# Expert tiles with one TensorE signal instead of four, down products two tiles behind, and the late scatters in one block

## What is computed

```python
logits = x @ router_w.T
probs = softmax(logits)
top_w, top_idx = top_k(probs, 2)
w_te = einsum('tk,tke->te', top_w, one_hot(top_idx, 8))
g = einsum('th,eih->tei', x, gate_w)      # I = 352, H = 128
u = einsum('th,eih->tei', x, up_w)
h = silu(g) * u
y = einsum('tei,ehi,te->th', h, down_w, w_te)
out = x + layernorm(y)
```

## Time and profile before

| | us |
|---|---|
| median of three runs (lowest, highest) | 591.68 (590.68, 592.72) |
| profiled execution, its span | 596.4 |
| TensorE busy in the span | 532.1 (89%) |
| ScalarE busy | 395.4 (66%) |
| VectorE busy | 375.9 (63%) |
| POOL busy | 349.7 (59%) |

### The profile page before, as it was taken

One profiled execution on the slowest core, in us unless ns is written; L12 is line 12 of the kernel. 1 busy time (PEld: TensorE's weight loads), 2 busy tenths in 40 slices (PEclk: granted clock), 3 DMA queues, 4 the chain that ended last, 5 costly groups with the idle time before them and its releaser, 6 DMA issues.

```text
span 596.4 us, 14609 instructions
## 1 busy us (share of the span) xinstructions
PE 532.1 (89%) x4952; PEld 395.0 (66%) x4969; DVE 375.9 (63%) x1095; ACT 395.4 (66%) x880; POOL 349.7 (59%) x449
## 2 busy tenths in 40 slices
PE   6989899899899899988899899999976899999981
PEld 5655455556566455655555666889976899999960
DVE  6824583965975947996847877527742365555347
ACT  3388989888978788869788696644531355555425
POOL 6104636545538885357877258487578555565545
PEclk9999999999999999999999999999996799999997
DMA  7245333213213322232734512212122203321174
GB/s 196 76 126 161 111 99 109 74 37 108 80 45 122 102 86 71 77 100 78 201 109 134 132 56 52 59 55 69 55 61 69 55 32 86 88 63 32 33 287 141
DMA packets 47016, 55.62 MB, mean 93 GB/s; under 512 B 7376, under 2 KB 41056, under 8 KB 44784
## 3 DMA queue, kind: packets, MB, share of 16 engines
q1 hardware_dynamic: 42624, 45.76, 26.7%
q0 software_dynamic: 4320, 8.92, 4.5%
HBM read 36.27 MB, written 18.92 MB: 93 GB/s over the span
## 4 chain that ended last, share of the span: by engine, by line
PE 56%; DVE 15%; ACT 10%; POOL 6%; issue 6%; DMA 3%; another core or an unknown queue 3%; DVEq 1%; SPq 0%; ACTq 0%; POOLq 0%
PE SC L871 11%; PE OA L748 9%; PE OA L881 6%; PE M L786 4%; PE M L822 4%; PE SC L730 3%; ACT arena L1015 3%; PE SC L734 2%; PE M L643 2%; DVE SS L1330 2%; PE SC L740 2%; PE M L662 1%; POOL slots L1782 1%; PE M L852 1%
## 5 line engine op out<-in xcount | busy, mean ns | idle before, releaser
L1015 ACT ACTIVATE arena<-SC 128x1024 f32<-128x1024 f32 x160 | 161.9, 1039 | 14.7 <-PE SC L735 11.8
L871 PE MATMUL SC<-arena 128*128 128x128 f32 (+1 forms) x852 | 111.5, 283 | 0.0
L871 PEld LDWEIGHTS SC<-arena 128*128 128x128 f32 (+1 forms) x852 | 104.0, 191 | 0.4 <-issue 0.3
L748 PE MATMUL OA<-arena 128*32 128x256 f32 (+1 forms) x1536 | 88.9, 349 | 6.6 <-DVE arena L455 2.8
L1782 POOL DMA_INDIRECT slots<-XBA,IDX x64 | 72.6, 1134 | 37.0 <-DVE IDX L1455 19.6
L1503 DVE TENSOR_TENSOR arena<-arena,SC 128x256 f32<-128x256 f32 (+1 forms) x142 | 43.7, 348 | 68.6 <-issue 24.6
L881 PE MATMUL OA<-arena 128*128 (+1 forms) x426 | 62.5, 284 | 12.9 <-issue 8.1
L748 PEld LDWEIGHTS OA<-arena 128*32 128x32 f32 x1536 | 39.2, 109 | 44.0 <-issue 22.8
L881 PEld LDWEIGHTS OA<-arena 128*128 128x128 f32 (+1 forms) x426 | 55.2, 198 | 15.4 <-issue 15.4
L454 POOL TENSOR_TENSOR arena<-arena 128x512 f32<-128x512 f32 x32 | 42.7, 1335 | 36.2 <-ACT arena L1015 35.6
L447 POOL TENSOR_TENSOR arena<-arena 128x512 f32<-128x512 f32 x23 | 31.2, 1356 | 48.9 <-ACT arena L1015 48.8
(11 more groups left out here) (244 smaller groups left out, 1086.0 us busy)
## 6 DMA issues: line engine op xcount, KB each, us to landing
arena<-parts SPq DMA_DIRECT2D x90, 192.0 KB
parts<-arena SPq DMA_DIRECT2D x16, 384.0 KB
arena<-ytok SPq DMA_DIRECT2D x8, 512.0 KB, 7.3
XGA<-slots SPq DMA_DIRECT2D x39, 65.0 KB
arena<-slots SPq DMA_DIRECT2D x32, 65.0 KB, 1.9
X<-in_L_attn_x SPq DMA_DIRECT2D x4, 512.0 KB, 5.1
out<-X SPq DMA_DIRECT2D x8, 256.0 KB, 2.5
arena<-parts SPq DMA_DIRECT2D x12, 96.0 KB
```

Source lines behind the costliest of these rows:

```text
L748: mm = pe.matmul(OA[32 * j:32 * j + 32, q0:q0 + n], vals[:, t, 32 * h:32 * h + 32], probs(j), start=first, stop=last, skip_group_check=True)
L871: mm = pe.matmul(SC[0:n, r % 2, 512 * m + P * c:512 * m + P * (c + 1)], WSEL[s % 4][:, I * m + i0:I * m + i0 + n], XGT[r % 2], start=True, ...
L1015: act.activation(EB[u], SC[:, n % 2, :], ACT.Exp).then_inc(exp_done, 1)
```

## The change

Every expert tile has one signal of TensorE, `tile_full`, at the end of its step. Step `s` holds the three gate products of tile `s`, the transpose of tile `s + 2`, two of three up products, the down products of tile `s - 2`, and the last up product with the signal. ScalarE waits for that signal once per step and then does `evac_x(s + 2)`, `evac_y(s - 2)` and the silu of tile `s`. `HTB` has three buffers in place of two. From tile 24 on, turned rows and results alternate between two banks each (`M0` and `M1S[0]`, `OA` and `M1S[1]`); up to tile 24 there is one of each, and the next use of it waits for the copy of the use before (`had_bank`). There are `STILES + 2` steps, not `STILES + 1`.

The scatters of batch 5 are single DMAs at eight positions from 2 to 15 of body 8. Those of batches 6 and 7 are all at position 3 of body 9, ahead of the hand-out of that position, and `put` is called two steps behind. Batch 7 has a buffer of its own, `XBL`.

```diff
+LATE5_AT = (2, 4, 6, 8, 10, 12, 14, 15)
+LATE67_AT = 3
+DOUBLE = 24
...
+        def turned(s):
+            return (M1S[0] if s >= DOUBLE and s % 2 else M0)[:, 0:P]
+        def result(s):
+            return (M1S[1] if s >= DOUBLE and s % 2 else OA)[:, 0:P]
+        def had_bank(s):
+            return s - 1 if s <= DOUBLE else s - 2 if s > DOUBLE + 1 else -1
...
-            def step(s, r, it):
-                if s + 1 < STILES:
-                    xt(s + 1, r + 1, 16 * (it + 1 + (r + 1) // RING))
-                if s < STILES:
-                    gu(s, r)
-                if s >= 1:
-                    down(s - 1, r + 1, woff(s - 1))
+            def step(s):
+                if s < STILES:
+                    pe.wait_ge(wsel_rdy, s + 1)
+                    pe.wait_ge(xt_rdy, s + 1)
+                    if s >= 2:
+                        pe.wait_ge(sg_rdy, s - 1)
+                    half(s, 0, range(NIC))
+                    if s + 2 < STILES:
+                        xt(s + 2)
+                    if s >= 2:
+                        pe.wait_ge(h_rdy, s - 1)
+                    mm = half(s, 1, range(NIC - 1))
+                if s >= 2:
+                    mm = down(s - 2)
+                if s < STILES:
+                    mm = half(s, 1, (NIC - 1,))
+                mm.then_inc(tile_full, 1)
...
             def step(s):
+                act.wait_ge(tile_full, s + 1)
+                if s + 2 < STILES:
+                    evac_x(s + 2)
+                if s >= 2:
+                    evac_y(s - 2)
                 if s < STILES:
+                    silu(s)
...
+                    if b == NB and n in LATE5_AT:
+                        scatter(NB - 3, LATE5_AT.index(n) // 2, (LATE5_AT.index(n) % 2,))
+                    if b == NB + 1 and n == LATE67_AT:
+                        for k in range(2 * T):
+                            scatter(NB - 2 + k // T, k % T)
                     for s in early_tile(b, n):
-                        if s >= 1:
-                            put(s - 1, (s - 1) % RING)
+                        if s >= 2:
+                            put(s - 2, (s - 2) % RING)
```

More of the change, by code:

```diff
@@ L853, in weights @@
                 mm.then_inc(wt_full, 1)
[L858 to L867, removed]
-                    pe.wait_ge(xt_rdy, s + 1)
[L869 to L873, removed]
@@ L875, in down @@
-            def down(s, r, off):
-                pe.wait_ge(h_rdy, s + 1)
-                if s >= 1:
[L879 to L886, removed]
@@ L888, in step, with xt @@
-            def step(s, r, it):
-                if s + 1 < STILES:
-                    xt(s + 1, r + 1, 16 * (it + 1 + (r + 1) // RING))
+            def xt(s):
+                r, it = s % RING, s // RING
+                pe.wait_ge(xg_in[r], 16 * (it + 1))
+                if had_bank(s) >= 0:
+                    pe.wait_ge(xt_rdy, had_bank(s) + 1)
+                elif s > 0:
+                    pe.wait_ge(*drained(NB + 1, "logits"))
+                    pe.wait_ge(*drained(NB + 1, "count"))
+                return pe.transpose(turned(s), XG[r][:, 0:D], IDN[:, :])
@@ new lines, in half, with down @@
+            def half(s, m, chunks):
+                for c in chunks:
+                    i0, n = IC[c]
+                    mm = pe.matmul(SC[0:n, s % 2, 512 * m + P * c:512 * m + P * (c + 1)], WSEL[s % 4][:, I * m + i0:I * m + i0 + n],
+                                   XGT[s % 2], start=True, stop=True)
+                return mm
+            def down(s):
+                off = weights_offset(pe, s)
+                pe.wait_ge(h_rdy, s + 1)
+                if had_bank(s) >= 0:
+                    pe.wait_ge(ys_rdy, had_bank(s) + 1)
+                for c, (i0, n) in enumerate(IC):
+                    mm = pe.matmul(result(s), HTB[s % 3][0:n, P * c:P * (c + 1)],
+                                   WALL[0:n, bass.ds(off + 2 * I + P * c, P)], start=c == 0, stop=c == NIC - 1)
+                return mm
@@ L908, in early @@
                     pe.wait_ge(table_rdy, 2)
-                step(s, s % RING, s // RING)
+                step(s)
             pe.wait_ge(const_rdy, 1)
@@ L995, in _ @@
             pe.wait_ge(table_rdy, 3)
-            for s in range(EARLY, STILES + 1):
-                step(s, s % RING, s // RING)
-            keep_busy(29)
+            for s in range(EARLY, STILES + 2):
+                step(s)
+            keep_busy(29, SC[:, 0, :])
             for b in BY_TENSOR:
@@ L1169, in _ @@
                     if b == NB and n == 0:
-                        evac_x(0, 0)
-                        step(0, 0)
+                        for s in range(2):
+                            act.wait_ge(xt_full, s + 1)
+                            evac_x(s)
+                        step(0)
                     if b == 0 and n in TABLE_AT:
@@ L1217, in _ @@
                         if s > 0:
-                            step(s, s % RING)
-            for s in range(EARLY, STILES + 1):
-                step(s, s % RING)
+                            step(s)
+            for s in range(EARLY, STILES + 2):
+                step(s)
             act.preload_act_table_set("natural_log_exp_and_others")
@@ L1511, in select, with step @@
                 dve.tensor_copy(WSEL[s % 4], WALL[:, bass.ds(weights_offset(dve, s), 2 * I)]).then_inc(wsel_rdy, 1)
-            def step(s, r):
+            def step(s):
                 if s + 2 < STILES:
                     select(s + 2)
-                hidden(s, r)
+                hidden(s)
             dve.memset(AE[:, :], 0.0)
@@ L1778, in scatter @@
                     pool.wait_ge(route_w, b // 2 + 1)
-                for k in range(2):
+                for k in choices:
                     if b >= NB - 4:
@@ L1826, in _ @@
                     for body in (b - 1, b):
-                        if body % 2 and body >= 3:
+                        if body % 2 and 3 <= body < NB:
                             for k in range(2 * T):
-                                if n + NU * (b - body) == POOL_AT[body >= NB][f"sc{k}"]:
+                                if (b < NB or k < T) and n + NU * (b - body) == PRE[f"sc{k}"]:
                                     scatter(body - 3 + k // T, k % T)
+                    if b == NB and n in LATE5_AT:
[3 more added lines that the diff above has]
+                            scatter(NB - 2 + k // T, k % T)
                     for s in early_tile(b, n):
-                        if s >= 1:
-                            put(s - 1, (s - 1) % RING)
-            for s in range(EARLY - 1, STILES):
+                        if s >= 2:
+                            put(s - 2, (s - 2) % RING)
+            for s in range(EARLY - 2, STILES):
                 put(s, s % RING)
```

77 lines of the change are left out of this document (40 added, 37 removed).

## The result

The change is slower. Its four runs have a median of 607.88 us (605.03 to 608.74), the kernel before 592.20 us on the same chip (590.68 to 595.68, four runs): a ratio of 1.0237, 95% interval 1.0203 to 1.0271, or 15.7 us. The forecast was 582.8 us.

The account below looks back on a forecast made before the run. It took TensorE signals held up by POOL's back-to-back transfers as the bound: 596.4 - 11.9 + 3.0 = 587.5 us of span, or 582.8 us keeping the 4.7 us distance to the median; range 578 to 588 (chance 0.50), 8 in 10 575 to 593.

Parts of the forecast that it names:

- What bounds the kernel: Tiles 20 to 29: back-to-back POOL transfers queue TensorE's signals, roughly one getting through per POOL step; 20.9 us lost.
- Part 1, L = 1.0 for a lone signal: In the hole, one signal per tile was taken to wait 1.0 us on average for the next opening between POOL steps.
- The gain of 11.9: In the hole: 20.9 us now lost, less 9.0 us of new loss from one signal per tile.
- The sum's count: Some 17 steps after the one-bank steps, until POOL catches up near 490 us, charged 0.3 us each: 5.1 us.
- The rival of the longer block: POOL back to back for 57 us, not 34, costs more than signals saved: some 598; chance 0.15, shared with no effect.
- Its own signs: Hole of 25 to 30 us, not 40; wrong if TensorE waits for the load of tile 33 or 40.
- Part 2, 3.0 us before the hole: Before the hole, table loads, routing and one-bank steps waiting for a step's end lose 3.0 us, bounds 0 to 6.
- the 1.3 booked back: Before the hole, TensorE's short waits for `hidden`, which gets a step more, were to shrink by an estimated 1.3 us.
- The load of tile 40, booked at nothing: Padding copies and this load come by 476 us, when step 38 wants it at the earliest: no cost.
- Part 3, the dense tile and the end: Tiles 29 to 70 keep 19 records and a signal costs TensorE nothing: zero; the end 0, within 0.5 us.
- The span as a whole: Whole kernel: 596.4 - 11.9 + 3.0 = 587.5 us of span, 8.9 less.
- From span to median: Span before lay 4.7 us above its runs' median; keeping that distance turned 587.5 into 582.8 us.

Follow-up runs that it names:

- e7: The kernel before with the pause's memset at 256 columns, not 128, and nothing else: 585.0 us, ratio 0.9798.
- e2: The kernel before with only the changed places of the late scatters, four signals per tile: 601.12 us, ratio 1.0020.
- e1: The change with the late scatters back at the places of the kernel before, one signal per tile: 610.4 us, ratio 1.0193 to the kernel before.
- e4: The change with the last slot table four positions earlier on VectorE: 603.78 us, ratio 1.0104 to the kernel before.
- e5: The change with the pause's memset at 256 columns, not 128: 597.17 us, ratio 1.0009 to the kernel before.
- e9: The kernel before with the pause of 256 columns and the last slot table four positions earlier: 584.61 us, ratio 0.9861.
- e10: The kernel before with the changed places of the late scatters and the pause of 256 columns: 588.28 us, ratio 0.9906.
- e6: The change with scatters at their old places, the pause of 256 columns and the last slot table four positions earlier: 593.87 us, ratio 0.9933 to the kernel before.
- e11: The change with scatters at their old places, the last slot table four positions earlier and a pause of 384 columns: 594.65 us, ratio 1.0040 to the kernel before.
- e12: The kernel before with the last slot table four positions earlier and a pause of 384 columns: 592.03 us, ratio 0.9973.
- e3: The change with the pause's memset issued twice ahead of each late scatter and hand-out: 616.93 us, ratio 1.0291 to the kernel before.

## Why the prediction was wrong

*What bounds the kernel*: right. Signals of TensorE that are held up while POOL issues its transfers make the hole; e7 takes 19.3 us off tiles 19 to 31 by touching POOL alone (and gives 4.7 back around it, 3.1 of it at tile 39, which now stands before the rows of tile 40 are there). Not "one for each POOL step", though: see the next point.

*Part 1, L = 1.0 for a lone signal*: **the step that failed.** It took the spacing of deliveries in the earlier trace rows, one for each POOL step, as a law, so that fewer signals would wait less. A signal may wait through many steps: 12.0 us with one signal per tile, 11.6 with four (e2). Some wait not at all: in the change the signals of tiles 22 to 25 took 0.04 us with POOL busy all along, most of its steps stretched to 1.5 to 1.8. So L is no constant near 1.0, and what moved it in these runs was the spacing of POOL's row (e7), not the number of signals queued. The rows had a hint: POOL's even 1.50 was a mean of 1.46 and of stretched steps. At tile 28 the change was 8.7 us ahead of before (463.9 against 472.6), as forecast in kind; at tile 31 it was 5.8 behind. The gain of 11.9 came out as 1.2. (The sum's count was loose as well: from 444 to 490 us at 2.3 us a step are 20 steps, not 17, 0.9 us more at its 0.3 each; small beside the miss.)

*The rival of the longer block* named the sign, with a price of up to 598 us. Its mean wait of 2.7 was passed at tiles 28 to 30. Its own cause, the 57 us row, is refuted in part: e1 has no block and is as slow within the intervals, e2 has it and is not slower. The measured 607.88 us lie past even its 598, so it had the direction and neither the cause nor the price.

*Its own signs*: "the hole between tiles 20 and 29 should take 25 to 30 us" was met, 25.1 us from end to end (39.9 before), because the hole had moved to tiles 30 and 31, just outside that window. "I am wrong if the load of tile 33 or 40 is what TensorE waits for" was met as well: it waits 3.0 us for that of tile 40.

*Part 2, 3.0 us before the hole*: right in kind, short in size: 5.0 to tile 19, in both traces of the change, and 2.1 more ahead of tile 0 in one of them. The one-bank steps of tiles 9 to 15 take some 2.49 us and not 2.11, as forecast (2.4) (starts of the same product in the change):

```profile
411.79 1.05 PE L893 MATMUL SC<-arena 128*96 128x128 f32 x8
...
414.29 1.05 PE L893 MATMUL SC<-arena 128*96 128x128 f32 x8
...
416.77 1.05 PE L893 MATMUL SC<-arena 128*96 128x128 f32 x8
```

From tile 9 to 14 they make 1.4 us against before, which has a few longer steps of its own there. Tiles 0 to 5 cost 1.1 us more, tiles 15 to 19 2.7; the 1.3 booked back did not come.

*The load of tile 40, booked at nothing*: wrong. The sum had it issued by 476; it waited for the slot table, which stands behind `hidden` in VectorE's order and so inherits every late signal, and the rows are wanted a tile earlier. It cost 4.9 us (31 to 40), and e4 gets 5 back between 37 and 40. The sum took scatters, padding copies and the ring of buffers as its last wait and not the table.

*Part 3, the dense tile and the end*: right. 30 tiles take 63.4 us with one signal each and 63.2 with four. The Trainium skill (TensorE: Matmul & The Clock Gate, The cost: per-tile semaphore tail) gives 26.3 ns per increment for the tail of a group of products; carried over to this stream as the prediction did, three increments fewer on 30 tiles would save 2.4 us (an estimate from that figure), and the trace does not agree.

*The span as a whole*: 607.0 measured, 587.5 forecast. Of these 19.5 us the gain that did not come makes 10.7, the load of tile 40 4.9, the part before the hole 4.1 (with the 2.1 ahead of tile 0); after tile 40 it is nothing within 0.2.

*From span to median*: the 4.7 us that were subtracted to come from 587.5 to 582.8 have no ground. In each profiled run since, the span lies 1.7 to 1.8 us under that same run's time (607.0 and 608.74 for the change), so the profile of before, 596.4, was of an execution of about 598 us (an estimate), above the median of its runs. Before varied from 589.6 to 599.2 us within one group of runs. That explains why the medians differ by 15.7 and the spans by 10.6.

Open: by what GpSimd's transfers hold TensorE's signals and those alone (in the trace of the change those of ScalarE and VectorE arrive in 0.01 us in the same stretch), and when within an even row one is let through. A longer memset spaces both POOL's instructions and its transfers, and no run parts the two.

## What to carry to other kernels

Where an engine waits and its releaser is "remote", take the time from the producer's last record to the consumer's start for each signal, tile by tile, and look at what a third engine does in between; the mean delay hides one of 12 us that costs everything. Before making fewer signals, try to make them arrive: the spacing of the transfers that hold them up is one constant, and 0.11 us more on each step gave 2.0%, while a deeper pipeline gave nothing, asked for rows a tile sooner and put every other engine's work behind the end of a step. A pause is paid for in the queue behind it: 0.11 us more was right here, 0.22 us more lost most of it and the change with a doubled pause was the slowest kernel of all.

## What the hardware showed that was not expected

- TensorE's semaphore signals, 0.04 us otherwise, were held for up to 12.0 us while GpSimd issued indirect transfers 1.46 us apart, and came through 0.8 us after the row ended. With four signals per tile the longest was 11.6 us.
- With steps of 1.57 us or more ScalarE got none over 1.3 us late in e5, e7 and e9 and none over 2.4 in e10. But e6, at 1.57, had one of 7.0 us. With 1.68 us or more the latest was 0.04 us in e11 and 1.0 in e12.
- GpSimd's memset of 128 columns takes 0.22 us, and 0.59 us beside VectorE's copy of weights, so a busy VectorE spaces GpSimd's transfers by itself, and one that waits for a late signal lets them close up. DVE and POOL of e3:

```profile
461.82 0.22 POOL L1825 MEMSET IDLE<- 128x128 f32 x1
462.01 0.53 DVE L1547 COPY arena<-arena 128x704 f32 x1
462.09 0.59 POOL L1826 MEMSET IDLE<- 128x128 f32 x1
```

  The Trainium skill (GPSIMD Engine Reference, 1. Specifications) has the two engines share GpSimd's SBUF interfaces, with contention for some kinds of VectorE's instructions; by that, the trace agrees: in before, from 433 us on, the memset stays at 0.22 us beside the products of `hidden` (38 times), one of whose inputs is in the bank `SC`, and takes up to 0.51 us beside the copy.
- A stalled TensorE also pays in clock: the granted clock of 460 to 480 us was 0.87 in the change, and after a wait of 3.37 us the six records of the gate products at 471.08 took 1.48 us, against 0.90 at 465.06 after one of 1.14.
